# A patch-embedding, attention and mixture-of-experts tower on one core: the stages in another order, and half 1's gates by way of DRAM

## What is computed

```python
h = patches(x) @ tokW.T + tok_b                        # 576 tokens, 768 -> 64
q, k, v = h @ Wq.T, h @ Wk.T, h @ Wv.T                  # per image, 36 tokens
s = softmax((q @ k.T - masked * 1e10) / 8, axis=queries)
h = layernorm(h + s @ v)
top2, idx = top_k(h @ gate_w + gate_b, 2)               # 16 experts
moe = sum over the two of softmax(top2) * (relu(h @ w1[e] + b1[e]) @ w2[e] + b2[e])   # 64 -> 128 -> 64
h = layernorm(h + layernorm(h + moe) * gamma + beta)
```

## Time and profile before

| | us |
|---|---|
| median of 3 runs (62.45 to 65.4) | 62.47 |
| the profiled execution's own time | 62.52 |
| its span, first to last instruction | 60.7 |

### The profile page before, as it was taken

One profiled execution on the slowest core, in us unless ns is written; L12 is line 12 of the kernel. 1 busy time (PEld: TensorE's weight loads), 2 busy tenths in 40 slices (PEclk: granted clock), 3 DMA queues, 4 the chain that ended last, 5 costly groups with the idle time before them and its releaser, 6 DMA issues.

```text
span 60.7 us, 1021 instructions
## 1 busy us (share of the span) xinstructions
PE 50.5 (83%) x377; PEld 27.8 (46%) x378; DVE 23.2 (38%) x90; ACT 23.7 (39%) x64; POOL 5.0 (8%) x23
## 2 busy tenths in 40 slices
PE   2999999999989999999999954999999999770000
PEld 0425538747625467746563623354675454150000
DVE  1041203234804935133806194054352381604620
ACT  1701030563268402825555062109640907714320
POOL 6998000000000000000000000000000000000000
PEclk9999999999999999999999999999999999999855
DMA  0799998710000000000000000000000000020002
GB/s 0 209 351 349 392 312 182 194 49 11 0 0 0 0 0 0 0 0 11 0 0 0 5 0 0 5 0 0 0 0 0 0 11 0 0 49 0 0 0 49
DMA packets 1915, 3.31 MB, mean 54 GB/s; under 512 B 757, under 2 KB 949, under 8 KB 1845
## 3 DMA queue, kind: packets, MB, share of 16 engines
q1 hardware_dynamic: 1830, 3.18, 17.5%
q10 hardware_dynamic: 80, 0.07, 0.4%
HBM read 3.09 MB, written 0.15 MB: 53 GB/s over the span
## 4 chain that ended last, share of the span: by engine, by line
PE 77%; DVE 9%; ACT 8%; issue 2%
PE banks L556 13%; PE banks L564 12%; PE banks L582 9%; PE banks L537 7%; PE banks L462 6%; PE banks L576 4%; PE banks L511 3%; PE banks L480 2%; PE banks L545 2%; PE banks L468 2%; PE banks L473 2%; PE banks L571 2%; PE banks L519 2%; ACT hid L252 2%; PE banks L492 2%; PE banks L486 2%
## 5 line engine op out<-in xcount | busy, mean ns | idle before, releaser
L252 ACT ACTIVATE hid<-banks 128x576 f32<-128x576 f32 x16 | 10.0, 645 | 10.3 <-PE banks L556 10.3
L385 DVE TENSOR_TENSOR xg<-banks,y1T 128x288 f32<-128x288 f32 x16 | 6.7, 453 | 13.8 <-PE banks L537 12.2
L556 PE MATMUL banks<-xg,w1c 64*128 64x288 f32 x64 | 10.2, 431 | 0.0
L564 PE MATMUL banks<-hid,w_sb 128*64 128x288 f32 x64 | 10.0, 422 | 0.0
L556 PEld LDWEIGHTS banks<-xg,w1c 64*128 64x128 f32 x64 | 5.6, 186 | 3.6 <-DVE xg L385 2.1
L582 PE MATMUL banks<-zeros 128*128 128x512 bf16 x17 | 5.9, 498 | 1.2 <-DVE zeros L405 1.2
L564 PEld LDWEIGHTS banks<-hid,w_sb 128*64 128x64 f32 x64 | 3.7, 135 | 4.7 <-issue 1.8
L537 PE MATMUL banks<-gT,sel 64*128 64x288 f32 x28 | 4.9, 425 | 0.0
L340 DVE TENSOR_REDUCE var<-sq 72x4 f32<-72x256 f32 x6 | 2.5, 414 | 5.5 <-ACT sq L225 5.5
L582 PEld LDWEIGHTS banks<-zeros 128*128 128x128 bf16 x18 | 1.9, 118 | 4.4 <-issue 2.5
L462 PE MATMUL banks<-xk,tokwb_sb 128*64 128x288 f32 x24 | 3.9, 447 | 0.0
(11 more groups left out here) (88 smaller groups left out, 58.2 us busy)
## 6 DMA issues: line engine op xcount, KB each, us to landing
xk<-x_kt SPq DMA_DIRECT2D x6, 288.0 KB, 4.5
w1x_sb<-w1x SPq DMA_DIRECT2D x1, 524.1 KB
w_sb<-w SPq DMA_DIRECT2D x1, 512.0 KB, 8.9
tokwb_sb<-tokw SPq DMA_DIRECT2D x1, 192.5 KB, 2.6
out<-fin SPq DMA_DIRECT2D x2, 72.0 KB
small_sb<-small ACTq DMA_DIRECT2D x1, 64.5 KB, 3.0
```

What stands on the lines that cost most here:

```text
L252: nc.scalar.activation(hid[:, h, 2 * p:2 * p + 2, :], p_hid[:, slot:slot + 2, :], ACT.Relu).then_inc(hid_ready, 1)
L385: nc.vector.tensor_tensor(xg[:, h, p, :], p_gb[p % GB], y1T[:, h, :], ALU.mult).then_inc(xg_ready, 1)
L556: mm = nc.tensor.matmul(p_hid[:, 2 * (p % RING) + r, :], w1c[rows, p, :], xg[rows, h, p, :], start=True, stop=True)
L564: mm = nc.tensor.matmul(p_moe[h][D * r:D * (r + 1), :], w2_sb[:, e, :], hid[:, h, e, :], start=(p == 0), stop=(p == PAIRS - 1))
```

## The change

It does seven things.

1. In half 1 the gates of pairs 2 to 7 are no longer spread by PE. SP waits for the second `gT_copy`, stores the 16 gate rows of half 1 (18 KB) into a DRAM scratch `gates`, waits for that store, and then fetches them with four DMAs that read each row 64 times, into the new tile `gb`: pairs 2 and 3 (two DMAs of 147 KB, one for each set of 64 partitions), and pairs 4 to 7 (two of 295 KB). `gate_tokens_fetched` multiplies from `gb`. `gates_spread(1, 0)` remains for pairs 0 and 1.
2. The order of stages is new on PE, ACT and DVE. Half 1's `residual` and `attend` come ahead of half 0's experts; the gamma and beta products come after `embed(1, 2)` and not inside `embed(0)`; `logits(1)` comes one pair earlier and `gates_transpose(1)` ahead of `experts_in(0, 6)`. On DVE `gates` is cut into `gates_top` and `gates_out`, with other work between.
3. `w1_centre` works in 4 groups of 256 columns, in other banks. The ten `keep_warm` products in the middle become three.
4. `values(1)` goes from DVE to ACT (one activation per tile), `yT_copy(0)` from ACT to DVE.
5. b2 moves from `small` into `w2` as a 17th block, and `experts_bias` contracts over all 128 partitions of `gT` (the added rows of b2 are zero) and no longer over 64.
6. The end of half 1 is cut in two parts of two tiles each (`ENDS`), with a combine bank, a layer-norm chain and an output DMA of their own.
7. `tokwb_sb` is issued by ACT ahead of `small_sb`, so that SP begins with `xk`.

```diff
-    WG = 2
-    PG = PAIRS // WG
+    PG = 2
+    WG = PAIRS // PG
+        gates = nc.dram_tensor("gates", (PAIRS, 2, HT), F32, kind="Internal").ap()
+        ENDS = ((0, 0, NT, p_cc[0]), (1, 0, NT // 2, p_cc[1]), (1, NT // 2, NT, p_cc[2]))
+        FETCHES = ((GB, 2 * GB), (2 * GB, PAIRS))
...
         def _(sp):
-            sp.dma_start(tokwb_sb[:, :], tokw).then_inc(tokw_in, 16)
...
+            sp.wait_ge(gT_ready, HALVES)
+            sp.dma_start(gates.rearrange("p r n -> (p r) n"), gT[0:E, 1, :]).then_inc(gates_stored, 16)
+            sp.wait_ge(gates_stored, 16)
+            for k, (p0, p1) in enumerate(FETCHES):
+                for r in range(2):
+                    sp.dma_start(gb[D * r:D * (r + 1), p0 - GB:p1 - GB, :],
+                                 gates[p0:p1, r, :].unsqueeze(0).to_broadcast([D, p1 - p0, HT])).then_inc(gb_in[k], 16)
...
+            def gate_tokens_fetched(p):
+                for k, (p0, p1) in enumerate(FETCHES):
+                    if p == p0:
+                        dve.wait_ge(gb_in[k], 32)
+                nc.vector.tensor_tensor(xg[:, 1, p, :], gb[:, p - GB, :], y1T[:, 1, :], ALU.mult).then_inc(xg_ready, 1)
...
+            def values(h):
+                act.wait_ge(srec_ready, h + 1)
+                act.wait_ge(v_psum, h + 1)
+                for t in range(NT):
+                    ins = nc.scalar.activation(vs[:, h, t, :], p_v[h][:, t, :], ACT.Copy, scale=srec[:, h, t:t + 1])
+                ins.then_inc(vs_ready, 1)
...
-                nc.tensor.matmul(p_moe[h][0:D, :], b2, gT[0:D, h, :], start=False, stop=False)
+                nc.tensor.matmul(p_moe[h][0:D, :], w2_sb[:, E, :], gT[:, h, :], start=False, stop=False)
...
-            keep_warm(2, 0)
-            pe.wait_ge(w1_ready, 1)
+            w1_centre(0)
             logits(0)
             w1_centre(1)
-            keep_warm(8, 0)
+            w1_centre(2)
+            w1_centre(3)
+            keep_warm(3, 5)
...
             combine(1)
+            combine(2)
```

More of the change, by code:

```diff
@@ L57, in vit_tower @@
         gatex = w1x_sb[:, E * F:E * F + E]
-        w2_sb = sb("w2_sb", [F, E, D])
-        wq, wk, wv, b2 = (small_sb[:, D * k:D * (k + 1)] for k in range(4))
-        gamma, beta = (small_sb[:, 4 * D + k:4 * D + k + 1] for k in range(2))
+        w2_sb = sb("w2_sb", [F, E + 1, D])
+        wq, wk, wv = (small_sb[:, D * k:D * (k + 1)] for k in range(3))
+        gamma, beta = (small_sb[:, 3 * D + k:3 * D + k + 1] for k in range(2))
         ident = sb("ident", [TT, TT])
@@ L280, in _ @@
             squares1(0)
-            inverse_deviation(0, 0)
+            inverse1(0)
+            exps(1)
             w1_copy(0)
-            yT_copy(0)
-            exps(1)
             gate_exp(0)
             w1_copy(1)
+            values(1)
+            w1_copy(2)
+            w1_copy(3)
+            squares1(1)
+            inverse1(1)
             gT_copy(0)
@@ L352, in y1_beta, with gates_top @@
                                         ALU.add).then_inc(yb_ready, 1)
-            def gates(h):
-                shape = [TT, NT, TOPK, E]
+            def gates_top(h):
                 dve.wait_ge(lg_psum, h + 1)
@@ L410, in _ @@
             nc.vector.tensor_copy(wv2[:, :], p_wv).then_inc(wv_ready, 1)
+            t_copy(0)
+            softmax_max(0)
+            sums_inverse(0)
+            values(0)
             dve.wait_ge(cgc_psum, 1)
@@ L422, in _ @@
             softmax_max(1)
-            gates(0)
+            yT_copy(0)
+            gates_top(0)
+            sums_inverse(1)
+            gates_out(0)
             gate_tokens(0, 0)
+            variance1(1)
             gate_tokens(0, 1)
-            values(1)
+            norm1_out(1)
             gate_tokens(0, 2)
             gate_tokens(0, 3)
-            variance(1, 0)
+            gates_top(1)
             gate_tokens(0, 4)
             gate_tokens(0, 5)
-            norm1_out(1)
+            gates_out(1)
+            dve.wait_ge(cgc_ready, 2)
+            y1_beta(0)
             gate_tokens(0, 6)
             gate_tokens(0, 7)
-            dve.wait_ge(cgc_ready, 2)
-            y1_beta(0)
-            gates(1)
-            for p in range(4):
-                gate_tokens(1, p)
-            moe_add(0)
-            gate_tokens(1, 4)
-            gate_tokens(1, 5)
-            variance(0, 1)
-            gate_tokens(1, 6)
-            gate_tokens(1, 7)
+            y1_beta(1)
+            gate_tokens(1, 0)
+            gate_tokens(1, 1)
+            gate_tokens_fetched(2)
+            gate_tokens_fetched(3)
+            moe_add(0)
+            gate_tokens_fetched(4)
+            gate_tokens_fetched(5)
+            variance(1, 0)
+            gate_tokens_fetched(6)
+            gate_tokens_fetched(7)
             norm2_out(0)
-            y1_beta(1)
-            variance(0, 2)
+            variance(2, 0)
             norm3_out(0)
             moe_add(1)
+            moe_add(2)
             variance(1, 1)
+            variance(1, 2)
             norm2_out(1)
-            variance(1, 2)
+            norm2_out(2)
+            variance(2, 1)
+            variance(2, 2)
             norm3_out(1)
+            norm3_out(2)
         @block.tensor
@@ L595, in _ @@
             embed(0, 0)
-            pe.wait_ge(gcen_ready, 1)
-            for r in range(2):
-                nc.tensor.matmul(p_cgc[D * r:D * (r + 1), :], cen2[0:D, :], gcen[:, :], start=True, stop=True)
-            nc.tensor.matmul(p_betac, bc(beta, [D, TT]), cen2[0:D, :], start=True, stop=True).then_inc(cgc_psum, 1)
             embed(0, 1)
@@ L611, in _ @@
             embed(1, 2)
-            mask_scores(1)
+            pe.wait_ge(gcen_ready, 1)
+            for r in range(2):
+                nc.tensor.matmul(p_cgc[D * r:D * (r + 1), :], cen2[0:D, :], gcen[:, :], start=True, stop=True)
+            nc.tensor.matmul(p_betac, bc(beta, [D, TT]), cen2[0:D, :], start=True, stop=True).then_inc(cgc_psum, 1)
             attend(0)
@@ L645, in _ @@
             experts_in(0, 3)
+            logits(1)
             gates_spread(0, 2)
@@ L669, in _ @@
             experts_in(1, 3)
-            gates_spread(1, 2)
             combine(0)
```

188 lines of the change are left out of this document (109 added, 79 removed).

## The result

The changed kernel takes 57.03 us (median of 4 runs, 56.20 to 57.73) where the kernel before takes 62.46; the ratio is 0.902, with a 95% interval of 0.898 to 0.907. All ratios in this document are taken over the shorter of the two groups that the runs of a kernel fall into. The forecast was 56.4, range 55.3 to 59.3. The profiled execution took 56.41 us for a span of 54.6. The four runs lie in two groups, 56.20 and 56.41 against 57.66 and 57.73.

A forecast was written before the change was run, and what follows sets the result against it. PE's work between 5.4 and 52.7 us, two waits for gates and the end's length bound the kernel; 0.64 + 3.07 + 1.36 + 1.0 = 6.07 us less than 62.52 gives 56.4 us, range 55.3 to 59.3.

The forecast's parts named there:

- Opening: Up to the end of embed(1): 0.69 us earlier, as gamma and beta products (0.53) and one turn (0.16) leave embed(0).
- To the first pair: From half 0's logits to its first expert product: experts_in(0, 0) starts at 22.88 instead of 23.52, 0.64 us earlier.
- E: Moment when residual(1) and attend(1) end on PE, forecast at 21.18 us; later than 21.7 would make the prediction wrong.
- Half 0's experts: experts_in(0, 0) to experts_in(1, 0): 3.07 us less than 16.69, from moved attention, no gate wait, fewer turns, a cheaper spread.
- Half 1's experts: experts_in(1, 0) to the end of experts_out(1, 7): net 1.36 us less than 12.49, if fetched gates arrive in time.
- a wait over 0.3 and a fetch over 2.5 us: Signs in half 1: first fetches land within 2.5 us, PE's wait for xg of pair 2 under 0.3.
- late fetch: Rival: half 1's fetched gates land later than taken and PE waits; 56.6 to 60.2 us, chance 0.18.
- The other estimate: By the skill page's DMA costs, half 1's first fetches make xg 0.3 us late, and the time 0.3 longer.
- The end: After the last expert product: 1.0 us less than 5.92, from half-length steps; the output's landing stays.
- Tight ACT and DVE queues: Rival: ACT and DVE queues tighter than drawn, delaying gates_top(1) and the end's two parts; 57.2 to 58.3 us, chance 0.16.
- Slower: Rival: PE idles so long for fetches that its clock drops in half 1; over 63.7 us, chance 0.03.

The follow-up runs named there:

- fetch-alone profile: Kernel before plus only the scratch fetch of half 1's gates for pairs 2 to 7, three spreads removed: 62.96 to 67.42 us, ratio 1.013; profiled execution 66.57 us.

## Why the prediction was right, and where not

The sum was right to 0.04 us in the profiled execution (6.11 us less, forecast 6.07). Its terms were not all right, and that they add up so well is luck: two came out 0.38 and 0.60 us too small, three 0.64, 0.15 and 0.2 too large, and these cancel.

- *Opening.* Forecast 0.69 us earlier at the end of `embed(0)`, measured 0.05 (7.95 for 8.00). The step that failed is the gamma and beta products and one turn that leave `embed(0)`, priced at their full duration. They lay beside a landing of `xk` (6.95 in the profile above) and a clock that was still coming up (5.99 us in the kernel before). The sentence that moving `tokwb_sb` to ACT costs nothing failed too: `small_sb` landed at 5.76, 0.97 later than PE's zero products ended. In the lower group this hides under the same landing and clock (55.9 to 56.4 us with either loading order); in the upper it costs 1.4 to 1.9 us, and it is why the median is 57.0 and not 56.4.
- *To the first pair.* The start of `experts_in(0, 0)` was forecast at 22.88 and came at 23.26, 0.26 earlier than before and not 0.64. `values(1)` took 0.93, forecast 0.95; the wait for it and the rest of the path moved with the opening. E came at 21.71, and by the prediction's own signs (an E later than 21.7) that is on the border.
- *Half 0's experts.* Forecast 3.07 less, measured 3.71 (12.98 for 16.69). The wait for half 1's gates went, as said. The missed 0.6 is in small things that the step did not list: the four spreads take 2.09 us and not 2.55, of which it had counted 0.2; `logits(1)` takes 0.40 and not 0.55 in the chain; the wait of 0.13 that it drew ahead of pair 4 is 0.04; and the first two pairs take 1.17 where they took 1.31, since the gates' transpose now stands between the second pair's spread and its product, which had waited for DVE.
- *Half 1's experts.* Forecast 1.36 less, measured 0.76. The gap of 0.25 behind the first relu came as drawn (0.3). The fetch did not: the store landed 1.44 us after its issue (forecast 1.75), but the first two fetches took 3.1 us in the median and not 2.4, and the issue of one took 0.66 and not 0.45. So `xg` of pair 2 came 0.44 us late, where the prediction had called a wait over 0.3 and a fetch over 2.5 us signs against it. The rival "late fetch" was true in its mild form, and cost half a microsecond. The other estimate in the prediction, 0.3 us late, came nearer in the total, but the last 0.3 in its sum (14.2 + 2.7 + 0.3) has no source, and without it `xg` would have been in time; it too put the landing 2.7 us after the issue, where 3.1 was measured. The fixed 2.0 us that it takes from the Trainium skill ("DMA: Bandwidth & Descriptors", Anatomy of one DMA) is a fit to transfers issued by GpSimd, and these came from SP, where the store of 18 KB landed in 1.44 us.
- *The end.* Forecast 1.0 less, measured 1.15 (4.77 for 5.92), and 0.2 more by the smaller last output, which the sum had left as it was.
- *The rivals.* Tight ACT and DVE queues did not show; no wait of PE in half 0 was over 0.1 us. "Slower" did not come, but both halves of its mechanism exist: in the fetch-alone profile a wait of 2.1 us is followed by the lower clock, and in the middle an idle stretch of 0.9 us is (no zero products there). I had read from the end of the kernel that the clock falls 1.8 to 3.3 us after PE's last work, and asked for fetches late by 5.5 us in sum before the whole would be slower. The kernel stood closer to that edge than the rows of before could tell: three zero products of 0.7 us hold it.

## What to carry to other kernels

Before you count a moved piece of work at its full duration, ask what lies beside it: in an opening, the landing of the next load and a clock still coming up can make it free where it stands. A fetch through DRAM (store, then read back with repeats) costs about 5.3 us from the data being ready to its arrival here (the store 1.4, an issue 0.7, the fetch 3.2); it pays when an order of stages gives it that time, and loses when not. Take filler products away only with a run beside it, since three of 0.7 us in sum held 3.5 us and more here, and look for two groups of times when a kernel's opening waits for a DMA.

## What the runs showed of the hardware that I had not expected

- The granted clock fell to 0.50 for ten microseconds after about 0.9 us of idling within two, and three 512-column products of zeros prevented it; a gap of 1.5 us elsewhere did not cause it. In the fetch-alone profile it fell twice, once with PE busy for 1.59 of the two microseconds before. The Trainium skill ("TensorE: Matmul & The Clock Gate", Part 1) says that the gate follows how busy PE has been of late; the fall from 1.00 to 0.50 behind the idle stretch agrees with that, while the fall at 19.2 us of the fetch-alone kernel is not told from the kernel before by it.
- The clock first came up between 3.96 and 7.23 us in eleven profiles and between 9.34 and 10.39 in three, and the same twelve instructions then take 1.61 us or 2.98. The printed column reads 1.00 before the first rise in all of them.
- A load of 48.5 KB that is second in ACT's queue behind one of 192.5 KB took 4.6 us to land, and 2.8 us when it was alone there.
- Reading 64 copies of each row out of DRAM ran at 246 GB/s in the fullest slices of the changed kernel's profile (up to 288 in its other profiles with all fetches from SP), against 359 to 422 for the plain loads.
